# Scaling the own keys' probabilities on ScalarE instead of VectorE in an attention kernel, with VectorE's loop turned one unit later

## The reference

```python
q, k = rope(rmsnorm(q, q_norm_w)), rope(rmsnorm(k, k_norm_w))
L = NPP * PSIZE                              # 16 pages x 32 = 512 cached keys
k_all = concat([k_cache[block_table], k])    # 512 cached + 32 own keys
v_all = concat([v_cache[block_table], v])
scores = einsum('bqhd,bkhd->bhqk', q, k_all) * SCALE
scores = where(valid, scores, -1e30)         # cached keys beyond the length
probs = softmax(scores)
o = einsum('bhqk,bkhd->bqhd', probs, v_all)
x = x + einsum('bse,de->bsd', o.reshape(bsz, seqlen, HQ * D), Wo)
```

## Time and profile before

| | |
|---|---|
| median of 3 executions | 2274.84 us (2274.13 to 2275.26) |
| the profiled execution, its own time | 2276.92 us |
| its span, first to last instruction | 2275.1 us |
| TensorE busy | 2229.5 us, 98% |
| VectorE busy | 1757.3 us, 77% |
| ScalarE busy | 1595.5 us, 70% |
| GpSimd busy | 600.0 us, 26% |
| DMA moved | 456.05 MB, 200 GB/s on the mean |

### The profile page before, as it was taken

The page is one execution under the profiler, slowest core; times in us unless marked ns, Lnnn a source line. Parts: engine busy times, 40 slices in busy tenths (PEclk is TensorE's granted clock), DMA queues, the critical chain, the costliest instruction groups (busy, mean ns, idle before and its releaser), DMA issues.

```text
span 2275.1 us, 57159 instructions
## 1 busy us (share of the span) xinstructions
PE 2229.5 (98%) x15424; PEld 1999.8 (88%) x15424; DVE 1757.3 (77%) x5602; ACT 1595.5 (70%) x4413; POOL 600.0 (26%) x907
## 2 busy tenths in 40 slices
PE   7999999999999899999999999999999999998999
PEld 6787888888887899999999999999999999997777
DVE  3433777777777999999899899899999999994332
ACT  4423666666666988888888888888888888884221
POOL 1003444444444222222222222222222222210000
PEclk9999999999999999999999999999999999999999
DMA  5335333333336888888788888888888888874332
GB/s 171 97 111 162 103 103 99 101 103 102 99 100 191 275 263 254 262 260 259 250 257 260 255 264 256 266 258 255 266 266 251 264 264 260 255 225 172 139 131 91
DMA packets 348137, 456.05 MB, mean 200 GB/s; under 512 B 34682, under 2 KB 281018, under 8 KB 343870
## 3 DMA queue, kind: packets, MB, share of 16 engines
q1 hardware_dynamic: 308430, 315.83, 44.6%
q0 software_dynamic: 36864, 134.23, 17.9%
q10 hardware_dynamic: 2672, 4.31, 0.5%
HBM read 374.54 MB, written 79.69 MB: 200 GB/s over the span
## 4 chain that ended last, share of the span: by engine, by line
PE 92%; DVE 2%; issue 2%; SPq 2%; DMA 1%; ACT 1%; ACTq 0%; DVEq 0%
PE oP L1285 18%; PE S L1252 16%; PE S L1209 12%; PE oP L1209 11%; PE bank L1139 9%; PE S L1303 8%; PE bank L1316 7%; PE oP L1139 3%; PE oP L1167 2%; PE oP L1295 2%; SPq L379 1%; PE oP L1159 1%; DVE k_lo L1000 1%; PE oP L1373 1%; PE bank L1269 1%
## 5 line engine op out<-in xcount | busy, mean ns | idle before, releaser
L1285 PEld LDWEIGHTS oP<-regC,regK 128*128 128x128 f32 x4096 | 529.4, 191 | 36.3 <-issue 4.9
L1285 PE MATMUL oP<-regC,regK 128*128 128x128 f32 x4096 | 540.5, 275 | 1.2
L731 ACT CAST k_hi<-regK 128x544 fp32r<-128x544 f32 x512 | 331.5, 647 | 127.7 <-PE S L1252 118.9
L1015 DVE CUSTOM_DVE_ANT_0 regC<-S,mask 128x544 f32<-128x544 f32 x512 | 369.0, 721 | 66.7 <-issue 59.0
L745 ACT ACTIVATE regC<-regC,nmx 128x544 f32<-128x544 f32 x512 | 388.0, 758 | 2.3 <-DVE nmx L1015 2.2
L1000 DVE TENSOR_TENSOR k_lo<-regK,k_hi 128x544 fp32r<-128x544 f32 x512 | 368.6, 720 | 12.7 <-ACT k_hi L731 12.7
L549 POOL COPY idx<-idx_all 128x1 int32 (+1 forms) x260 | 70.3, 273 | 963.2 <-PE oP L1295 652.0
L570 POOL TENSOR_TENSOR regC<-regC 128x256 f32<-128x256 f32 x320 | 245.4, 788 | 279.3 <-DVE regC L975 278.3
L1139 PE MATMUL bank<-ident,regC 128*128 128x128 f32 x2048 | 307.3, 272 | 2.8 <-ACT regC L791 2.8
L791 ACT COPY regC<-bank 128x512 f32<-128x512 f32 x512 | 298.7, 583 | 5.0 <-PE bank L1139 5.0
L552 POOL DMA_INDIRECT regK<-v_cache,idx x256 | 269.8, 1054 | 115.0 <-issue 114.2
(11 more groups left out here) (138 smaller groups left out, 4295.9 us busy)
## 6 DMA issues: line engine op xcount, KB each, us to landing
regK<-kT_cache SPq DMA_DIRECT2D x1024, 128.0 KB
qkT_d<-regC SPq DMA_DIRECT2D x160, 256.0 KB, 2.3
regC<-qkT_d SPq DMA_DIRECT2D x64, 512.0 KB, 6.3
oT_d<-regC SPq DMA_DIRECT2D x64, 256.0 KB
regK<-oT_d SPq DMA_DIRECT2D x16, 1024.0 KB, 5.4
regC<-wqk SPq DMA_DIRECT2D x10, 1024.0 KB, 5.2
v_d<-regC SPq DMA_DIRECT2D x32, 256.0 KB, 2.3
regK<-qkT_d SPq DMA_DIRECT2D x64, 128.0 KB
```

Source lines behind the costliest of these rows:

```text
L731: nc.scalar.copy(k_hi[u % 2].rearrange("p (s t) -> p s t", t=PSIZE), k_sb[b][:, :, h, :]).then_inc(s_khi, 1)
L1015: nc.vector.tensor_tensor_reduce(out=p_sb[u % 4], in0=scores, in1=mask[:], scale=-SCALE, scalar=3e38, op0=ALU.add, op1=ALU.min, accum_out= ...
L1285: last = nc.tensor.matmul(oP[:, at:at + P], v_sb[b][:, m, h * D:(h + 1) * D], pT_sb[u % 2][:, m * P:(m + 1) * P], start=(h < 4 and m == 0) ...
```

## The change

It does two things. The multiplication of the 32 own columns by `rinv` moves from VectorE (`normalise`, line 1026) to ScalarE, as `own_scaled(n, u)` between `split_k` and the copy of `pT` in ScalarE's step, 512 times in all. It writes the same numbers to the same place; `turn_own` gets a wait for ScalarE's new semaphore `s_own` beside the one on `s_evA`. And VectorE's loop over the groups is closed one unit later (`TURN` 7 instead of 6).

```diff
-TURN = 6
+TURN = 7
...
+            def own_scaled(n, u):
+
+                act.wait_ge(s_ri, n + 1)
+                j = u % 4
+                nc.scalar.activation(po_sb[u // 4 % 4][:, j * C:(j + 1) * C], p_sb[j][:, L:KW], ACT.Copy,
+                                     scale=rinv[:, j:j + 1]).then_inc(s_own, 1)
...
                 if u % HK != 1 and not (fixed and n + 4 >= NU):
                     split_k(n + 4, u + 4, g * 2 + (u + 4) // (2 * HK))
+                own_scaled(n, u)
                 act.wait_ge(s_ta, n + 1)
                 ge(act, s_pv, n - 1)
                 nc.scalar.copy(pT_sb[u % 2], pT).then_inc(s_evA, 1)
...
             def normalise(n, u):
                 dve.wait_ge(s_ri, n + 1)
                 p, j = p_sb[u % 4], u % 4
-                nc.vector.tensor_scalar(po_sb[u // 4 % 4][:, j * C:(j + 1) * C], p[:, L:KW], rinv[:, j:j + 1], None, ALU.mult)
                 nc.vector.tensor_scalar(p[:, 0:L], p[:, 0:L], rinv[:, j:j + 1], None, ALU.mult).then_inc(s_p, 1)
...
             def turn_own(g, u):
 
+                pe.wait_ge(s_own, g * UG + u + 1)
                 pe.wait_ge(s_evA, g * UG + u + 1)
```

More of the change, by code:

```diff
@@ L277, in build @@
         s_qhi, s_qp = sem("s_qhi"), sem("s_qp")
-        s_mask, s_qk, s_mx, s_exp, s_ri, s_p = (sem(f"s_{x}") for x in ("mask", "qk", "mx", "exp", "ri", "p"))
+        s_mask, s_qk, s_mx, s_exp, s_ri, s_p, s_own = (sem(f"s_{x}") for x in ("mask", "qk", "mx", "exp", "ri", "p", "own"))
         s_ta, s_tb, s_evA, s_evB = sem("s_ta"), sem("s_tb"), sem("s_evA"), sem("s_evB")
```

## The result

The changed kernel takes **2288.99 us** in the median (2286.94 to 2292.03), the kernel before 2274.49 (2270.72 to 2275.26) beside it. The ratio is 1.0070, with a 95% interval of 1.0059 to 1.0082. It is 14.5 us slower. The prediction had 2277.7 with a range up to 2281: it was wrong, in its time and in what it held likeliest, which was no measurable change.

What follows compares the result with a forecast made beforehand. TensorE was taken to bound the kernel, VectorE part of group 0. One scaling's slip in 15 groups (+3.3 us) and group 0 (-0.4) gave +2.9 on 2274.84, hence 2277.7 us, range 2273.5 to 2281.

Steps and rivals of the forecast that it cites:

- no measurable change: Whole kernel: time within 0.2% (4.5 us) of before, with a lean to slower; chance 0.76.
- The price of the scaling: ScalarE, each of 512 units: one 128x32 scaling takes 0.22 us from start to start, between 0.13 and 0.32.
- The taut chain at the head of a group: Unit 2: ScalarE's high key part, VectorE's low part and maximum, TensorE's scores, without slack; 0.22 us later in 15 groups, +3.3 us.
- No slip at units 3 and 4: Early in a group: the later copy of `pT` still precedes the next transposes, at unit 3 by 0.09 us.
- The relief of VectorE: VectorE gains 0.15 us a unit; it counts only in group 0, at most 5.1 us, partly lost waiting for ScalarE's weight split.
- The turn at unit 7: VectorE's loop branch stays covered by queued instructions: nothing either way; 2.7 us if the cover were gone.
- the long stretch: 1109 to 2035 us, where TensorE bounds: VectorE some 50 us less busy, ScalarE 70 to 80 more.
- it catches up: From unit 4 on TensorE's units exceed 2.08 us while ScalarE needs 2.0, so ScalarE's lateness shrinks and each group slips once.
- all else on TensorE follows: After the scores load 0.22 us late at a group's head, TensorE's later work shifts equally, since nothing else there is idle.
- the term for the wait on `s_own`: TensorE, 64 times ahead of the own transposes: nothing, queued behind eight `values` matmuls; bare, at most 0.13 us each, 8 us.
- Group 0: First group, where VectorE bounds 757 to 796 us: -0.4 us taken, between -5.1 and +1.
- The rival on the slower side: Slower by over 0.2%: scaling price high enough that `pT` copies decide (2281 us), or a bare `s_own` wait; chance 0.19.

Runs made afterwards that it cites:

- the one without the wait in the best order: Changed kernel with the scaling ahead of the key split, behind it at u % 8 = 1, and the `s_own` wait moved from TensorE to ScalarE once per batch: 2274.34 us.

## Why the prediction was wrong

**Right, by its own steps.** The price of the scaling: 0.21 to 0.22 from start to start and 0.32 long, as worked out from the activation of 128x4. The taut chain at the head of a group: +0.21, and 1.64 us between the two loads where 1.65 was written. No slip at units 3 and 4 in the changed kernel, though the room there was as thin as the prediction said: with the order changed (`u` = 4, +0.16) or the scaling doubled it came. The relief of VectorE: small, and in part turned into a wait for ScalarE's half of the split. The turn at unit 7 cost nothing by itself. In the long stretch VectorE is 52 us less busy, as forecast; ScalarE is 58 us busier, where 70 to 80 was forecast.

**The step that failed** is "it catches up" and, before it, that all else on TensorE follows. It checked the copy of `pT` against the next transposes at units 2 and 3, and then let ScalarE's idle time (88.0 us) stand for the rest. But the copy has a second reader. `turn_own` wants it in its own unit, behind the eight loads of `values`, where the next transposes come behind the own ones and a whole score as well, at four places in each group. The text named those transposes as queued behind the wait on `s_own`, and the wait for the copy as one that is "waited for anyway"; it did not ask by how much the copy was early. It was early by 0.115 us, less than the 0.21 of the scaling. And the term for the wait on `s_own`, "nothing", was wrong as well. That wait costs 0.11 us between the copy and the next scores. Its cost is hidden at 48 of 64 places only as long as the copy is on time, and it used up the copy's room. The two together left the whole price of the scaling on the path: 0.20 four times a group, 0.80, and 0.11 more at the branch. With the forecast 3.3 us for the chain, 0.80 x 15 = 12.0 us and 0.11 x 15 = 1.6 us for the branch make 16.9 us for the groups 1 to 15, against 15.6 counted (the last group ends before its fourth such place counts, and small differences of 0.01 take the rest). By the length of a group, the experiment with the scaling early at the last units took 0.77 x 15 = 11.6 us back, and the one without the wait in the best order 0.11 x 15 = 1.6.

**Group 0** was forecast at -0.4 and came out at +1.1. By eights of its units it is +0.43, +0.16, +0.24 and +0.27. Unit by unit the relief is there: eleven units are 0.11 to 0.21 shorter, 1.7 us together. Nine units (7, 10, 12, 16, 18, 19, 24, 26 and 31) are 0.14 to 0.37 longer, 2.2 us together. Unit 1 (+0.5) says little, since it moves by 0.3 and 0.2 between profiles of kernels that do not differ there. The run with the scaling early at the last units has group 0 at 85.42, 0.7 less, which is the part of the ends of batches, and still 0.4 above the kernel before. Three of the nine (12, 16 and 18) are 0.14 to 0.16 longer also where nothing is scaled at all. That the rest is ScalarE's later parts was not run by itself.

**The rival on the slower side** was given 0.19, for a price over 0.27 or a bare wait. The price stayed at 0.21 to 0.22. The bare wait did happen, on TensorE's path at the ends of batches once the copy was late, at 0.11 us each by the sums above, within the 0.13 that the prediction allowed for it and gave little weight. The other half of the loss, the late copy itself at the ends of batches, is in neither way of the rival.

**The loop turn** was judged by what covers the branch on its own engine ("nothing, either way"), and 2.7 us if the cover were gone. For the kernel as changed that held. The reason didn't: with the body 32 instructions shorter the turn at unit 6, where it was before, would have cost 105 us, and no row of the kernel before shows it. `TURN` = 7 is no adornment of the change but a part that it needs.

## What to carry to other kernels

For every result that an instruction is moved ahead of, list all its readers, and for each take the time from the producer's end to the reader's start: where it is little above the shortest that any trace has for such a pair (0.12 us in the kernel before, 0.05 in the run without the second wait), what little room there is will not hold a new instruction, also where the trace shows no idle time. Count a second wait as part of the new work: it can be free alone, because it fits into the room, and still cost in full beside another change that needs the same room. Idle time counts only if it lies behind the last wait that stands ahead of the new work; total it by place and not by engine. And after any edit that changes the length of a hardware loop, compare the packets of the instruction queue: 65 more of them were 105 us.

## What the runs showed of the hardware

- A turn of VectorE's loop can cost 4 to 7.5 us each time, by the place of the body in its program alone. Moving the body by 8 records makes it go away. The sign is idle time "issue" behind the branch with all semaphores reached, and packets in the instruction queue that grow with the turns (5 each).
- A 128x32 activation with a per-partition scale lasts 0.32 us and takes 0.21 to 0.22 us of ScalarE. Two in a row take 0.43, so nothing more is saved by pairing them.
- One more waiting instruction on TensorE is free as long as the result of the other wait is early enough (the wait alone, at 48 of 64 places). It costs 0.11 us where that result comes last (0.34 instead of 0.225 us from the copy to the next scores), and in front of a loop branch that is not covered.
- From the end of a copy on ScalarE to the weight load that waited for it, it is 0.05 us with one wait and 0.11 with two (medians over the groups 2 to 13).
